# Second mixture of experts: router worked by chunks inside the last block, first expert's row by TensorE, accumulators opened early, chunks turned back through four banks

## Chip, cores and metric

One core of one Trainium2 chip runs the whole program as one launch. The metric is the device time of that launch in microseconds, before and after the change, as the median of several runs.

## The reference, cut to what matters

Two layers, each an attention part and an expert part, on 2048 tokens of width 128. The change is in the second layer, from the last block to the end, and in two places of the first layer's experts.

```python
# L1_attn: 8 blocks, scanned: linear attention, then feed forward, each with residual and layernorm
x = _layernorm(attn + residual, ln1_s, ln1_b)
h = gelu(x @ Wf1 + bf1); ff = gelu(h @ Wf2 + bf2)
x = _layernorm(ff + residual, ln2_s, ln2_b)
# L1_ffn: 8 experts, top 2 of a softmax router, no capacity
scores = softmax(x2d @ gate_w.T)
h = silu(xe @ w1[e]) * (xe @ w3[e]);  out = out + h @ w2[e]        # hidden width 352
# around them
x = x + ga * _L1_attn_ref(h, ...)
h = _layernorm(x, axis=-1) * (1 + cb) + sb
x = x + gb * _L1_ffn_ref(h, ...)
```

## The kernel before

The tokens are 16 tiles of 128, in four chunks (NC = 4) of four tiles. X and XN hold tokens on the partitions, HT holds features on the partitions. PS is the accumulator memory of TensorE, eight banks of 512 columns. Every engine has its own instruction stream, written out by hand in the order in which it runs; semaphores join them. Names: PE is TensorE, v is VectorE (DVE), a is ScalarE (ACT), g is GpSimd (POOL), sp is SyncE, which issues the loads and stores in its queue's order.

The last block (`pe_body`, `act_body`, `v_body`) goes through the chunks m = 0 to 3. A chunk has a first product with gelu (HF, `pe_f1`), a second (`pe_f2`), G2B from ScalarE, the sum Y2 on VectorE (L1927), four transposes to tokens (`pe_t2`), statistics (`v_stats`), the power -1/2 on GpSimd, the normalisation (`v_apply`), four transposes back (`pe_u2`) and scale and bias into HT (`act_x2`). The steps of one chunk's end lie between those of the next.

When all four chunks are in HT, the second expert part begins, with each step for all chunks before the next:

1. sixteen transposes of HT back to tokens (L1717) and the additions to X on VectorE (L2260);
2. the norm: statistics on VectorE (`norm_stats`), `norm_rstd` on GpSimd, `norm_apply` on ScalarE, four transposes into bank 7 (`norm_turn`), scale and bias into HT (`norm_feat`); bank 7 is one, so the chunks follow each other;
3. router products of all 16 tiles into bank 4 (`pe_router`), copied by VectorE (`v_logits`), then the choice of two experts on VectorE (`v_route1`), giving wt;
4. wt turned by TensorE, copied to wtT and stored to device memory (scr_w). Each expert's row of weights, 16 x 128 numbers, is then loaded from there to all partitions, into SB1 (`sp_row1`, 1 MB);
5. meanwhile TensorE opens the four accumulators with a product by zero (`pe_moe1`).

The loop over experts follows: GpSimd multiplies HT by the row into XS (L2046), TensorE makes the two products (L2074, L2075), ScalarE silu, VectorE the product HG, TensorE the third product into the accumulator of the chunk. 8 experts, 4 chunks and 3 pieces of hidden width make 96 tiles. At the end `act_back` copies the accumulators to OT, `pe_back` turns a chunk into bank 7 when VectorE has taken the one before, `v_last` adds it to X, and SP stores it.

The first layer's experts end in the same `pe_back`, and begin with `pe_route0` (one small product that counts tokens per expert) and `pe_row0`, by which the row of the first expert is spread by TensorE and copied by ScalarE and VectorE.

## Time and profile before

| | us |
|---|---|
| median of 3 runs | 2030.13 (2030.09 to 2036.85) |
| profiled execution, its own time | 2029.81 |
| its span | 2028.1 |
| TensorE busy | 1723.4 (85%) |
| VectorE busy | 1358.1 (67%) |
| ScalarE busy | 1159.0 (57%) |
| GpSimd busy | 290.5 (14%) |

The shares are means over stages that have different limits. The chain that ended last lies for 55% of the span on TensorE, 30% on VectorE, 7% on ScalarE and 3% in loads. Blocks run from about 1202 to 1715 us, the second expert loop from 1769 to 2018. Times below are from the start of the span, in us. A TensorE product in f32 with 512 columns appears as two instructions (two passes), a transpose as one.

### The profile page before, as it was taken

How to read it: one execution, taken by the hardware profiler on the slowest of the kernel's cores; microseconds unless marked ns; L12 is line 12 of the kernel's file. 1: busy time of each engine (PE TensorE's matmuls, PEld its weight loads, DVE VectorE, ACT ScalarE, POOL GpSimd, SP SyncE). 2: the span in 40 equal slices, each digit the busy share in tenths (PEclk: the TensorE clock that was granted, in tenths of full speed). 3: DMA queues.
4: the chain of work that ended last, by engine and by line, in shares of the span. 5: the costliest groups of instructions: out<-in, count | busy, mean ns of one | idle time of the engine just before them, and what ended most of it. 6: DMA issues, size and time to landing. Idle time of an engine off the chain costs nothing.

```text
span 2028.1 us, 28151 instructions
## 1 busy us (share of the span) xinstructions
PE 1723.4 (85%) x10382; PEld 768.5 (38%) x10382; DVE 1358.1 (67%) x2666; ACT 1159.0 (57%) x2106; POOL 290.5 (14%) x384
## 2 busy tenths in 40 slices
PE   5798058799999999999969948888988887499998
PEld 3798055122222222222344424444444443244443
DVE  6998876999999999999343355656656565122222
ACT  5565003298999999999823355666656664222222
POOL 4465002300000000000000021111111112011110
PEclk8999578599999999999979969999999999599999
DMA  1000000112000000000114200000000000211340
GB/s 50 1 2 1 0 0 9 48 31 38 2 2 2 2 2 1 2 2 2 33 33 88 68 0 1 16 16 16 16 1 16 16 0 1 59 36 46 49 58 25
DMA packets 74590, 40.15 MB, mean 20 GB/s; under 512 B 22128, under 2 KB 70768, under 8 KB 74464
## 3 DMA queue, kind: packets, MB, share of 16 engines
q1 hardware_dynamic: 73888, 37.70, 9.2%
q8 instruction: 77, 1.26, 0.3%
q10 hardware_dynamic: 576, 0.79, 0.1%
q14 instruction: 49, 0.40, 0.1%
HBM read 35.13 MB, written 3.15 MB: 19 GB/s over the span
## 4 chain that ended last, share of the span: by engine, by line
PE 55%; DVE 30%; ACT 7%; issue 4%; DMA 3%; SPq 1%; POOL 1%; DVEq 0%; ACTq 0%; POOLq 0%
DVE MX L1130 17%; PE PS L1642 6%; PE PS L1648 5%; PE PS L1212 5%; PE PS L2074 4%; PE PS L2075 4%; PE PS L2084 4%; PE PS L1238 3%; PE PS L1593 3%; DMA SB<-scr_w 3%; PE PS L525 2%; PE PS L1612 2%; PE PS L1089 2%; DVE MS L629 2%; PE PS L1484 2%
## 5 line engine op out<-in xcount | busy, mean ns | idle before, releaser
L1271 ACT ACTIVATE tmpb<-PS 128x512 f32<-128x512 f32 x1024 | 554.2, 595 | 75.6 <-PE PS L1238 56.5
L1130 DVE TENSOR_REDUCE MX<-PS 128x2 f32<-128x1024 f32 x512 | 584.4, 1215 | 17.6 <-PE PS L1089 15.5
L1212 PE MATMUL PS<-tmpb,VS 128*32 128x256 f32 x4096 | 327.7, 392 | 1.5 <-ACT tmpb L1271 0.6
L1089 PE MATMUL PS<-KST,QST 56*128 56x512 bf16 x1024 | 205.6, 400 | 18.5 <-DVE MX L1130 16.7
L1238 PE MATMUL PS<-QST,KST 59*128 59x512 bf16 x1024 | 200.5, 388 | 3.6 <-DMA QST<-NMP 0.6
L2109 DVE TENSOR_TENSOR HG<-HG,PS 128x512 f32<-128x512 f32 (+1 forms) x96 | 65.9, 686 | 199.5 <-PE PS L2075 199.5
L2099 ACT ACTIVATE HG<-PS 128x512 f32<-128x512 f32 (+1 forms) x96 | 57.2, 596 | 208.0 <-PE PS L2074 208.0
L1212 PEld LDWEIGHTS PS<-tmpb,VS 128*32 128x32 f32 x4096 | 80.8, 108 | 196.0 <-issue 108.0
L1238 PEld LDWEIGHTS PS<-QST,KST 59*128 59x128 bf16 x1024 | 49.4, 92 | 222.2 <-ACT tmpb L1271 208.8
L1642 PE MATMUL PS<-X,WF 128*128 128x512 f32 x256 | 128.3, 636 | 4.2 <-ACT X L1787 4.2
L1803 ACT ACTIVATE HF<-PS,CL 128x512 f32<-128x512 f32 x128 | 88.0, 687 | 68.5 <-PE PS L1642 68.5
L1648 PE MATMUL PS<-HF,WF 128*128 128x512 f32 x256 | 116.4, 592 | 0.0
L2074 PE MATMUL PS<-XS,G 128*128 128x512 f32 (+1 forms) x192 | 99.1, 597 | 12.2 <-POOLq L2048 12.2
L1900 DVE TENSOR_SCALAR N<-PS,BA,RR 128x128 f32<-128x128 f32 x256 | 85.9, 403 | 25.7 <-POOL RR L1946 14.4
L1927 DVE TENSOR_TENSOR Y<-G2B,X 128x512 f32<-128x512 f32 x32 | 22.1, 692 | 119.1 <-ACT G2B L1811 119.1
L2075 PE MATMUL PS<-XS,G 128*128 128x512 f32 (+1 forms) x192 | 98.6, 595 | 0.0
L2084 PE MATMUL PS<-HG,G 128*128 128x512 f32 (+1 forms) x192 | 96.8, 592 | 0.0
L525 PE MATMUL PS<-BIG,ident 128*128 128x128 f32 x512 | 66.5, 285 | 29.4 <-DVE BIG L460 29.4
L1593 PE MATMUL PS<-HT,WA 128*128 128x512 f32 x192 | 90.6, 605 | 0.1
L1507 DVE TENSOR_TENSOR HID<-HID,SB 128x512 f32<-128x512 f32 x64 | 42.6, 689 | 70.1 <-ACT HID L1496 38.4
L1184 POOL TENSOR_SCALAR NG<-MM 128x16 f32<-128x16 f32 x16 | 4.1, 254 | 550.0 <-DVE MM L1136 550.0
L1946 POOL TENSOR_TENSOR RR<-VE,mhalf 128x4 f32<-128x4 f32 x32 | 38.4, 1198 | 307.9 <-DVE VE L1893 307.9
(326 smaller groups left out, 2549.1 us busy)
## 6 DMA issues: line engine op xcount, KB each, us to landing
SB<-scr_w SPq DMA_DIRECT2D x15, 1024.0 KB, 14.9
WF<-in_L_attn_Wf SPq DMA_DIRECT2D x16, 256.0 KB, 3.0
QST<-NMP SPq DMA_DIRECT2D x192, 1.0 KB
G<-in_L_ffn_w SPq DMA_DIRECT2D x16, 176.0 KB, 2.4
W<-in_L_ffn_w SPq DMA_DIRECT2D x16, 128.0 KB, 2.1
QST<-scr_q SPq DMA_DIRECT2D x14, 128.0 KB
scr_q<-tmpb SPq DMA_DIRECT2D x3, 512.0 KB, 3.6
KST<-scr_k SPq DMA_DIRECT2D x14, 96.0 KB
```

The lines of the kernel that those rows point to most:

```text
L525: pe.matmul(PS[:, x, 0:HH * SCOL], ident[:, :], PR[:, i, heads(x), :].rearrange("p h c -> p (h c)"), start=i == 0, stop=False, skip_group_ ...
L1089: pe.matmul(PS[:, b + x, :], QST[r, 2 * g + jj, CH * qc + P * t:CH * qc + P * t + P], KST[r, g, cs(kc)], start=True, stop=True).then_inc(s ...
L1130: r = v.tensor_reduce(MX[:, :, m // (TPC * NC), m // NC % TPC, m % NC], PS[:, b:b + 2, :], AX.X, ALU.max)
L1212: last = pe.matmul(PS[32 * j:32 * j + 32, 3, h], VS[:, kt, u // NC, :], PB[:, kt % 2, j, h], start=(kt == 0 and half == 0), stop=(kt == NT ...
L1238: pe.matmul(PS[:, (at + x) % 3, :], KST[r, g, P * kt:P * kt + P], QST[r, 2 * g + jj, cs(qc)], start=True, stop=True).then_inc(s_qk, 1)
L1271: a.activation(PB[:, kt % 2, j, :], PS[:, at % 3, :], ACT.Exp, scale=HD ** -0.5).then_inc(s_exp, 1)
L1593: pe.matmul(PS[:, bank, :], WA[:, b % 2, j, :], HT[:, cs(c)], start=True, stop=True).then_inc(done, 1)
L1642: pe.matmul(PS[:, 3 + j % 2, :], WF1[:, b % 2, P * j:P * j + P], X1[:, n % 2, :], start=True, stop=True).then_inc(s_f1, 1)
L1648: f = pe.matmul(PS[:, 5, :], WF2[:, b % 2, j, :], HF[:, j, :], start=(j == 0), stop=(j == KF - 1))
L2074: pe.matmul(PS[0:w, b, :], G1[:, k, f:f + w], XS[:, c % 2, :], start=True, stop=True).then_inc(s_h, 1)
L2075: last = pe.matmul(PS[0:w, b + 1, :], G3[:, k, f:f + w], XS[:, c % 2, :], start=True, stop=True)
L2084: pe.matmul(PS[:, c, :], G2[0:w, k, m, :], HG[0:w, o % 4, :], start=False, stop=False, skip_group_check=True).then_inc(s_hfree, 1)
```

## The change

The chunks of the second expert part are worked inside the last block: transposes back (`pe_out1`), addition (`v_out1`), statistics (`v_stat1`), the power alone on GpSimd (`norm_pow`), the normalisation on VectorE (`v_norm_apply`), turning (`pe_turn1`), scale and bias (`act_feat1`) and router products (`pe_logits1`). The accumulators are opened right behind the router's last product (`pe_sums1`). The first expert's row is spread by TensorE (`pe_row`, now for both expert parts), so one row load falls away. `pe_back` uses the banks 4 to 7 for the chunks, in both expert parts. `pe_route0` gets three products whose result nobody reads. The gate's eight small loads stand earlier in SP's queue.

```diff
+        def norm_pow(g, S_, k, c):
+            g.wait_ge(S_["stat"], upto(k, c))
+            g.tensor_tensor(rs[:, ts_(c)], vh[:, ts_(c)], mhalf[:, ts_(c)], ALU.pow).then_inc(S_["rstd"], 1)
+
+        def v_norm_apply(v, S_, src, k, c):
+            v.wait_ge(S_["rstd"], upto(k, c))
+            for t in tiles(c):
+                last = v.tensor_scalar(XN[:, t, :], src[:, t, :], ag[:, t, 0:1], rs[:, t:t + 1], ALU.subtract, ALU.mult)
+            last.then_inc(S_["normed"], 1)
...
@@ def pe_route0
             pe.matmul(PS[:, 6, 0:8], below[:, :], r["two"][:, 0, :], start=True, stop=True).then_inc(r["s_cntd"], 1)
+            for _ in range(3):
+                pe.matmul(PS[:, 7, :], ident[:, :], HT[:, cs(0)], start=True, stop=True)
             pe_weights(pe, r)
...
@@ def pe_back
                 pe.wait_ge(s_oc, NC * n + c + 1)
-                if n or c:
-                    pe.wait_ge(s_y, NC * n + c)
                 for j, t in enumerate(tiles(c)):
-                    last = pe.transpose(PS[:, 7, P * j:P * j + P], OT[:, P * t:P * t + P], ident[:, :])
+                    last = pe.transpose(PS[:, 4 + c, P * j:P * j + P], OT[:, P * t:P * t + P], ident[:, :])
...
@@ def sp_blocks
+            for e in range(E1):
+                sp.dma_start(gate1[:, e:e + 1], A["L1_ffn_gate_w"][e].rearrange("(p a) -> p a", a=1)).then_inc(R1["s_in"], 16)
...
@@ def pe_body
                 else:
+                    if b == NB - 1:
+                        pe_out1(pe, 0)
                     pe_f2(pe, b, m, range(KF // 2))
                     pe_u2(pe, n + m - 1)
                     pe_f2(pe, b, m, range(KF // 2, KF))
                     if b < NB - 1:
                         pe_k(pe, b + 1, 0)
+                    else:
+                        pe_out1(pe, 1)
                 pe_t2(pe, n + m)
...
             else:
+                pe_turn1(pe, 0)
+                pe_out1(pe, 2)
+                pe_logits1(pe, 0)
+                pe_turn1(pe, 1)
                 pe_u2(pe, n + NC - 1)
+                pe_logits1(pe, 1)
+                pe_out1(pe, 3)
+                pe_turn1(pe, 2)
+                pe_logits1(pe, 2)
+                pe_turn1(pe, 3)
+                pe_logits1(pe, 3)
+
+        def pe_out1(pe, c):
+            pe.wait_ge(s_bx2, NC * (NB - 1) + c + 1)
+            if c == 3:
+                pe.wait_ge(s_x3, 1)
+            for j in range(TPC):
+                x = pe.transpose(PS[:, c % 3, P * j:P * j + P], HT[:, CH * c + P * j:CH * c + P * j + P], ident[:, :])
+            x.then_inc(s_bxt, 1)
...
@@ def v_body
+                if b == NB - 1 and m == NC - 1:
+                    v_out1(v, chain, 0)
+                    v_stat1(v, chain, 0)
+                    v_out1(v, chain, 1)
+                    v_norm_apply(v, SM, X, 5, 0)
                 v.wait_ge(s_g2, n + m + 1)
...
@@ def v_blocks
                 else:
+                    v_stat1(v, chain, 1)
                     v_stats(v, chain, 1, 6, s_t2, s_ep2, NC * NB - 1)
+                    v_norm_apply(v, SM, X, 5, 1)
                     v_apply(v, 1, 6, N2, s_r2, s_u2, s_n2, NC * NB - 1)
+                    v_out1(v, chain, 2)
+                    v_stat1(v, chain, 2)
+                    v_out1(v, chain, 3)
+                    v_stat1(v, chain, 3)
+                    v_norm_apply(v, SM, X, 5, 2)
+                    v_norm_apply(v, SM, X, 5, 3)
...
@@ sp_moe1
             sp_weights(sp, R1)
-            for k in range(2):
-                sp_row1(sp, k, k)
+            sp_row1(sp, 1, 1)
...
@@ tensor's program
             pe_blocks(pe)
-            for c in range(NC):
-                norm_turn(pe, SM, 5, c, (SM["feat"], 5 * NC + c) if c else (s_bx2, NC * NB))
-            pe_router(pe, R1, 6 * NC, 16 + 16 * E1)
+            pe_sums1(pe)
             pe_weights(pe, R1)
+            pe_row(pe, R1)
             pe_moe1(pe)
             pe_back(pe, 1, OT1)
```

The order of instructions shows it at three places. First TensorE in the last chunk of the last block, before the change. L1642 is the first product, L1648 the second, L1612 a turn of N (to features) or of Y (to tokens), L1717 the transposes back:

```order
L1642 MATMUL PS<-X,WF 128x512 [waits s_hf] x2
L1648 MATMUL PS<-HF,WF 128x512 [waits s_hf] x2
L1612 MATMUL PS<-ident,N 128x128 [waits s_bx2,s_n2]
L1612 MATMUL PS<-ident,N 128x128 x3
L1648 MATMUL PS<-HF,WF 128x512 [waits s_hf] x2
L1612 MATMUL PS<-ident,Y 128x128 [waits s_y2]
L1612 MATMUL PS<-ident,Y 128x128 x3
L1612 MATMUL PS<-ident,N 128x128 [waits s_bx2,s_n2]
L1612 MATMUL PS<-ident,N 128x128 x3
L1717 MATMUL PS<-ident,HT 128x128 [waits s_bx2]
L1717 MATMUL PS<-ident,HT 128x128 x3
```

And with the change, where L1716 is `pe_out1` and L1724 is `pe_turn1`:

```order
L1649 MATMUL PS<-X,WF 128x512 [waits s_hf] x2
L1716 MATMUL PS<-ident,HT 128x128 [waits s_bx2]
L1716 MATMUL PS<-ident,HT 128x128 x3
L1655 MATMUL PS<-HF,WF 128x512 [waits s_hf] x2
L1619 MATMUL PS<-ident,N 128x128 [waits s_bx2,s_n2]
L1619 MATMUL PS<-ident,N 128x128 x3
L1655 MATMUL PS<-HF,WF 128x512 [waits s_hf] x2
L1716 MATMUL PS<-ident,HT 128x128 [waits s_bx2]
L1716 MATMUL PS<-ident,HT 128x128 x3
L1619 MATMUL PS<-ident,Y 128x128 [waits s_y2]
L1619 MATMUL PS<-ident,Y 128x128 x3
L1724 MATMUL PS<-ident,XN 128x128 [waits s_normedM]
```

The transposes of chunks 0 and 1 now stand ahead of and behind the second product, and the first turn of the norm ahead of the last turn of N.

Second VectorE around the last Y2 sum, before:

```order
L1900 TENSOR_SCALAR N<-PS,BA,RR 128x128 x3
L1927 TENSOR_TENSOR Y<-G2B,X 128x512 [waits s_t2,s_g2]
L1888 BN_STATS BS<-PS 128x6 [waits s_t2]
L1888 BN_STATS BS<-PS 128x6 x3
L1891 BN_AGGR BA<-BS 128x2 [waits ch_v]
```

With the change, L2006 being `v_out1`, L130 to L140 the statistics and L160 the normalisation:

```order
L2006 TENSOR_TENSOR X<-X,PS 128x512 [waits s_bxt]
L130 BN_STATS st<-X 128x6 [waits ch_v]
L130 BN_STATS st<-X 128x6 x3
L133 BN_AGGR ag<-st 128x2 [waits ch_v]
L133 BN_AGGR ag<-st 128x2 x3
L140 TENSOR_SCALAR vh<-ag 128x4 [waits ch_v]
L2006 TENSOR_TENSOR X<-X,PS 128x512 [waits s_bxt]
L160 TENSOR_SCALAR XN<-X,ag,rs 128x128 [waits ch_v,s_rstdM]
L160 TENSOR_SCALAR XN<-X,ag,rs 128x128 x3
L1981 TENSOR_TENSOR Y<-G2B,X 128x512 [waits s_t2,s_g2]
```

Four steps (the addition of chunk 0, its statistics, the addition of chunk 1, the normalisation of chunk 0) stand ahead of the sum that the block waits for.

Third TensorE between router and expert loop, before (L1308 router, L1336 turn of wt, L2061 accumulators):

```order
L1308 MATMUL PS<-gate,HT 128x8 [waits s_featM,s_rin]
L1308 MATMUL PS<-gate,HT 128x8 x15
L1336 MATMUL PS<-ident,wt 128x128 [waits s_rw]
L2061 MATMUL PS<-zero,ident 128x512 [waits s_zero,s_rpd]
L2061 MATMUL PS<-zero,ident 128x512 x3
```

With the change (L1731 router, L2131 accumulators, L1337 turn of wt, L1456 the row):

```order
L1731 MATMUL PS<-gate,HT 128x8 x3
L2131 MATMUL PS<-zero,ident 128x512 [waits s_zero]
L2131 MATMUL PS<-zero,ident 128x512 x3
L1337 MATMUL PS<-ident,wt 128x128 [waits s_rw]
L1456 MATMUL PS<-wtT,ident 128x128 [waits s_rpd]
L1456 MATMUL PS<-wtT,ident 128x128 x15
L2138 UNCONDITIONAL_BRANCH [waits s_sb0]
```

The accumulators moved ahead of the routing's result, and sixteen products of the row came behind it.

## Rows read from the trace of the kernel before

**Rows 1.** The chain of waits, 1714 to 1771 us: start, length, engine, line.

```profile
1714.95 2.58 PE PS L1717 x12
...
1736.57 6.98 PE PS L1308 x32
...
1752.57 14.91 DMA SB<-scr_w
1767.55 1.27 POOL XS L2046
1769.01 2.04 PE PS L2074 x2
```

**Rows 2.** Busy time by stretch: PE, PEld, DVE, ACT, POOL, granted clock, DMA, GB/s.

```profile
1700.00:1760.00 60.00, 29.84 (x102) 19.52 (x101) 20.33 (x88) 17.22 (x30) 8.14 (x15) 0.66 0.12 28
```

**Rows 3.** TensorE in order of time, last chunk: start, length, line, operation, idle before.

```profile
1699.93 3.79 PE L1642 MATMUL PS<-X,WF 128*128 128x512 f32 x8
...
1705.71 1.88 PE L1648 MATMUL PS<-HF,WF 128*128 128x512 f32 x4
```

**Rows 4.** VectorE in order of time, last chunk and routing.

```profile
1708.35 0.69 DVE L1927 TENSOR_TENSOR Y<-G2B,X 128x512 f32<-128x512 f32 x1 [4.22 <-ACT G2B L1811]
1709.79 0.89 DVE L1888 BATCH_NORM_STATS2 BS<-PS 128x6 f32<-128x128 f32 x4 [0.75 <-PE PS L1612]
...
1712.42 1.37 DVE L1900 TENSOR_SCALAR N<-PS,BA,RR 128x128 f32<-128x128 f32 x4 [1.12 <-POOL RR L1950]
...
1743.57 0.29 DVE L1316 COPY L<-PS 128x128 f32<-128x128 f32 x1 [19.05 <-PE PS L1308]
...
1749.75 0.29 DVE L1997 TENSOR_TENSOR wt<-one,m 128x128 f32<-128x128 f32 x1
```

**Rows 5.** ScalarE and GpSimd in order of time, two steps of the passage.

```profile
1735.65 0.78 ACT L172 ACTIVATE HT<-PS,modc 128x512 f32<-128x512 f32 x1 [1.27 <-PE PS L166]
...
1711.37 1.01 POOL L1950 TENSOR_TENSOR RR<-VE,mhalf 128x4 f32<-128x4 f32 x1 [8.64 <-DVE VE L1893]
```

**Rows 6.** TensorE and VectorE in order of time, first experts' routing.

```profile
1038.64 0.39 PE L1413 MATMUL PS<-two,below 128*128 128x8 f32 x2 [1.51 <-DVEq L1396]
1041.54 0.40 PE L1336 MATMUL PS<-ident,wt 128*128 128x128 f32 x1 [2.51 <-DVE wt L1407]
1042.50 6.68 PE L1453 MATMUL PS<-wtT,ident 128*128 128x128 f32 x32 [0.55 <-DVEq L1342]
1050.11 3.67 PE L1477 MATMUL PS<-HT,W 128*128 128x512 f32 x8 [0.93 <-DVE SB L1463]
...
1041.19 0.29 DVE L1407 TENSOR_TENSOR wt<-t,m 128x128 f32<-128x128 f32 x1
```

**Rows 7.** VectorE and ScalarE in order of time, ends of both expert parts.

```profile
1166.21 0.69 DVE L2246 COPY Y<-PS 128x512 f32<-128x512 f32 x1 [3.25 <-PE PS L1520]
...
1171.81 0.69 DVE L2246 COPY Y<-PS 128x512 f32<-128x512 f32 x1 [1.33 <-PE PS L1520]
...
2018.13 2.42 ACT L1527 ACTIVATE OT<-PS,modc 128x512 f32<-128x512 f32 x4 [2.84 <-PE PS L2084]
...
2019.57 0.69 DVE L2116 TENSOR_TENSOR X<-X,PS 128x512 f32<-128x512 f32 x1 [3.26 <-PE PS L1520]
...
2024.98 0.69 DVE L2116 TENSOR_TENSOR X<-X,PS 128x512 f32<-128x512 f32 x1 [1.27 <-PE PS L1520]
```

**Rows 8.** GpSimd in order of time, first multiplication of the seventh expert.

```profile
1950.83 1.27 POOL L2046 TENSOR_TENSOR XS<-HT,SB 128x512 f32<-128x512 f32 x1 [10.36 <-DMA SB<-scr_w]
```

**Rows 9.** Busy time by stretch of 2 us, columns as in group 2.

```profile
1040.00:1042.00 2.00, 0.40 (x1) 0.14 (x1) 1.33 (x7) 0.00 (x0) 0.00 (x0) 0.92 0.00 0
1042.00:1044.00 2.00, 1.50 (x7) 1.51 (x8) 0.27 (x1) 0.00 (x0) 0.00 (x0) 0.50 0.11 33
...
1716.00:1718.00 2.00, 2.00 (x12) 1.77 (x10) 1.67 (x3) 0.00 (x0) 0.00 (x0) 0.62 0.00 0
1738.00:1740.00 2.00, 2.00 (x11) 2.00 (x11) 0.00 (x0) 0.00 (x0) 0.00 (x0) 0.50 0.00 0
```

More of the change, by code:

```diff
@@ L1292, in router @@
             r.update({n: sb(f"{n}{tag}", [P, NT], F32, stack) for n in ("m", "k")})
-            if nth == 1:
-                r["gate"], r["L"] = gate0, logit0
-            else:
-                r["gate"] = sb(f"gate{tag}", [P, E], F32, stack)
-                r["L"] = sb(f"L{tag}", [P, NT, E], F32, stack)
+            r["L"] = logit0 if nth == 1 else sb(f"L{tag}", [P, NT, E], F32, stack)
             r["wtT"] = sb(f"wtT{tag}", [P, P], F32, stack)
@@ L1301, in router @@
             return r
-        def pe_router(pe, r, feat, arrived):
-            pe.wait_ge(r["s_in"], arrived)
-            pe.wait_ge(SM["feat"], feat)
-            for t in range(NT):
-                last = pe.matmul(PS[:, 4, 8 * t:8 * t + 8], HT[:, P * t:P * t + P], r["gate"][:, :], start=True, stop=True)
-            last.then_inc(r["s_mm"], 1)
         def bc(ap):
@@ L1686, in pe_body, with pe_turn1, pe_logits1 @@
             else:
+                pe_turn1(pe, 0)
+                pe_out1(pe, 2)
+                pe_logits1(pe, 0)
+                pe_turn1(pe, 1)
                 pe_u2(pe, n + NC - 1)
+                pe_logits1(pe, 1)
[11 more added lines that the diff above has]
+            x.then_inc(s_bxt, 1)
+        def pe_turn1(pe, c):
+            pe.wait_ge(SM["normed"], upto(5, c))
+            if c >= 2:
+                pe.wait_ge(SM["feat"], upto(5, c - 2))
+            for j, t in enumerate(tiles(c)):
+                x = pe.transpose(PS[:, 3 + c % 2, P * j:P * j + P], XN[:, t, :], ident[:, :])
+            x.then_inc(SM["turned"], 1)
+        def pe_logits1(pe, c):
+            pe.wait_ge(R1["s_in"], 16 + 16 * E1)
+            pe.wait_ge(SM["feat"], upto(5, c))
+            for t in tiles(c):
+                x = pe.matmul(PS[:, 5, E1 * t:E1 * t + E1], HT[:, P * t:P * t + P], gate1[:, :], start=True, stop=True)
+            if c == NC - 1:
+                x.then_inc(R1["s_mm"], 1)
         def pe_inputs(pe, b):
@@ L1713, in pe_blocks @@
                 pe_body(pe, b)
-            for c in range(NC):
-                pe.wait_ge(s_bx2, NC * (NB - 1) + c + 1)
-                for j in range(TPC):
-                    x = pe.transpose(PS[:, c, P * j:P * j + P], HT[:, CH * c + P * j:CH * c + P * j + P], ident[:, :])
-                x.then_inc(s_bxt, 1)
         KGROUPS = (slice(0, 1), slice(1, 3), slice(3, 4))
@@ L1823, in act_blocks, with act_feat1 @@
                 else:
+                    act_feat1(a, 0)
+                    act_feat1(a, 1)
                     act_x2(a, b, NC - 1)
+                    act_feat1(a, 2)
+                    act_feat1(a, 3)
+        def act_feat1(a, c):
+            a.wait_ge(SM["turned"], upto(5, c))
+            a.activation(HT[:, cs(c)], PS[:, 3 + c % 2, :], ACT.Identity, scale=modc[:, 1, 4:5], bias=modc[:, 1, 3:4]).then_inc(SM["feat"], 1)
         def v_k(v, chain, b, g):
@@ L2020, in sp_moe1 @@
         def sp_moe1(sp):
-            for e in range(E1):
-                sp.dma_start(R1["gate"][:, e:e + 1], A["L1_ffn_gate_w"][e].rearrange("(p a) -> p a", a=1)).then_inc(R1["s_in"], 16)
             for k in range(2):
@@ L2169, in _ @@
             g.memset(zero[:, :], 0.0).then_inc(s_zero, 1)
-            for c in range(NC):
-                norm_rstd(g, chain, SM, 5, c, False)
             g.wait_ge(SM["feat"], 6 * NC)
@@ L2193, in _ @@
             act_blocks(a, Chain(a, ch_a))
-            for c in range(NC):
-                norm_apply(a, SM, X, 5, c)
-                norm_feat(a, SM, 5, c, modc[:, 1, 4:5], modc[:, 1, 3:4])
             act_route1(a, R1)
+            for c in (0, 2):
+                act_row(a, R1, SB1, c)
             act_moe1(a)
@@ L2210, in _ @@
             pe_route0(pe, R0)
-            pe_row0(pe, R0)
+            pe_row(pe, R0)
             pe_moe0(pe)
@@ L2257, in _ @@
             v_blocks(v, chain)
-            for c in range(NC):
-                v.wait_ge(s_bxt, c + 1)
-                v.tensor_tensor(X[:, ts_(c), :], X[:, ts_(c), :], PS[:, c, :].rearrange("p (t d) -> p t d", t=TPC),
-                                ALU.add).then_inc(s_x3, 1)
-            v.wait_ge(s_x3, NC)
-            for c in range(NC):
-                norm_stats(v, chain, SM, X, c, 1e-5, False)
             v_route1(v, chain, R1)
+            for c in (1, 3):
+                v_row(v, R1, SB1, c)
             v_moe1(v)
```

48 lines of the change are left out of this document (31 added, 17 removed).

## Prediction

> **What bounds the kernel now.** I read the chain of waits first, then each engine in order of time between 1698 and 1772 us, then the granted clock of that stretch. The span is 2028.1 us, the profiled execution's own time 2029.81, so 1.7 us lie around the span; the median of the runs shown is 2030.13, 0.3 above it. Inside the blocks and inside the expert loops the change moves nothing, so only four seams count: the start and the end of the first experts' loop, the passage from the last block to the second experts' loop, and the end of the kernel.
>
> The passage is the large one. The last feed-forward product of the blocks ends near 1707.6 [rows 3], and the second experts' first product starts at 1769.01 [rows 1]. In between TensorE is busy half of the time at a mean clock of 0.66 [rows 2]. The chain runs through sixteen transposes, norm statistics, four rounds of "normalise, turn, scale" one after another, 6.98 us of router products, 6.5 us of routing on VectorE (copy at 1743.57, weights ready at 1749.75 + 0.29 = 1750.04) [rows 1, 4], a write to device memory, and then 14.91 us in which everything waits for the first expert's row of weights [rows 1]. No other wait of the passage is so long.
>
> **Part by part. First the passage as far as the router's result.** Before, VectorE stands idle for 4.22 us ahead of the last Y2 sum at 1708.35 [rows 4]. The change puts chunks 0 and 1 there. TensorE turns chunk 0 back behind the first product of chunk 3, four transposes: 0.86 us at half clock (2.58 for twelve [rows 1]), 0.44 at full, so the second product ends 0.44 later. VectorE adds chunk 0 from about 1704.4 (0.69, the same form as the adds of [rows 7]) and takes its statistics (1.5 us, from 1709.79 until GpSimd starts at 1711.37 [rows 4, 5]), to 1706.6. The addition of chunk 1 waits for its transposes, which stand behind the second product: about 1708.6 to 1709.3. Then chunk 0 is normalised on VectorE. Four tensor_scalar of 128x128 take 1.37 us from PSUM [rows 4]; this form, with SBUF as source, isn't in the trace, so I bound it by that row above and, below, by the 0.69 that one instruction over the same 512 elements takes [rows 7], and take 1.1, nearer to the four short ones. Y2 therefore starts near 1710.4: 2.05 us late, and who waits for it is the last chunk of the block. Its statistics stand behind those of chunk 1 too (1.5 us) and start near 1712.6 against 1709.79; after GpSimd (1.0 [rows 5]) and the normalisation of chunk 1, its own follows at 1715.15 against 1712.42 [rows 4]: the block's last chunk is 2.7 us late.
>
> From there two things run beside each other. TensorE has by then had little to do and I expect the half clock: four transposes 0.86 us, router products of a chunk 1.75 (6.98 / 4). TensorE: turn of chunk 1 to 1716.2, the last chunk's turn to 1717.6, router products of chunk 1 to 1719.4, and only then the transposes of chunk 3, to 1720.4. VectorE: add to 1721.3, statistics to 1722.8, normalise chunk 2 to 1723.9 and chunk 3 to 1724.9. Last come turn (0.9 and 0.2 of latency), scaling on ScalarE (0.78 [rows 5]) and router products (1.75) of chunk 2, then the same of chunk 3: the scaling of chunk 3 waits for a turn that stands behind chunk 2's router products. 1723.9 + 1.1 + 0.8 + 1.8 + 1.1 + 0.8 + 1.8 is 1731.3. VectorE copies the logits at 1731.4 instead of 1743.57: **12.2 us**. At full clock all of this tail would end near 1727.2, for 16.3.
>
> **The accumulators.** Four zero products (eight passes, 3.8 us at full clock by the row at 1699.93 [rows 3], twice that at half) now lie beside the 6.5 us of routing. If the clock rises in the middle they are done before the weights, else up to 0.7 us late. I take 0.1.
>
> **The first row by TensorE.** Before, from weights ready to first product: 1769.01 - 1750.04 = 18.97 us [rows 1, 4]. The first experts' loop already does what is now planned: weights ready 1041.48, first product 1050.11, so 8.63 us [rows 6]; here GpSimd's multiplication is added (1767.55 to 1769.01: 1.46 [rows 1]), 10.1 together. That is with 32 row passes in 6.68 us at half clock (granted clock 0.50 from 1042 [rows 6, 9]). At full clock they take half, and the whole 6.8. The zero products keep TensorE busy until 1 or 2 us before the weights are ready, so I take the full clock: 18.97 - 6.8, **12.1 us**; at half 8.9.
>
> **Start of the loop.** It opens at half clock: the first pair of passes takes 2.04 us [rows 1], where a quarter of [rows 3]'s eight is 0.95. About 1.8 us are lost before the clock rises. Now row passes run until 2.4 us ahead of it. I take half, **0.9**, bounds 0 and 1.8.
>
> **Three warming products in the first routing.** TensorE has only 0.39 us of work at 1038.64 between two idle times of 1.5 and 2.5 us, and the clock falls just before the row passes (0.92 on average in 1040 to 1042, 0.50 after) [rows 6, 9]. Three products are six passes, 2.6 us at full clock: they begin at about 1038.9 and end at 1041.5, when the weights are ready (1041.48). The passes then take 3.4 instead of 6.68: **3.2 us**. If the clock fell all the same the gain is 0; if the warming products ran at half clock they would end at 1044.0 and cost 2.5. The loop behind depends on row loads that its own progress issues, so it moves as a whole.
>
> **Four banks instead of one.** After the first experts VectorE copies the four chunks from 1166.21 on, the last at 1171.81 [rows 7], so 1.9 us apart on average, since TensorE waits for each copy. With four banks they follow each other at 0.7, so the last starts at 1168.3: **3.5 us**, all on the path to the norm. At the end of the kernel likewise: ScalarE's four copies end at 2020.55, VectorE's sums start at 2019.57 and 0.65 apart, the last at 2021.5 instead of 2024.98 [rows 7]: 3.5. The four stores of the output get closer together; what stands between the last sum and the end (2028.1 - 2025.67 = 2.4) may grow a little: **3.4**.
>
> **Costs of nothing.** The gate's eight loads leave the queue of SP between chunk and expert loads and go ahead of block 2, where SP waits for the blocks anyway. GpSimd loses the negated means; its zero fill stays hidden under the norms. The copies to SBUF of the row are in the 8.63.
>
> Sum: 12.2 - 0.1 + 12.1 + 0.9 + 3.2 + 3.5 + 3.4 = 35.2; 2029.8 - 35.2 = 1994.6, plus 0.3 for the median: **1995**.
>
> **Rivals.** (a) *The clock lets a row down.* Idle times of 1 to 2.4 us stand ahead of each row and of the loop; an idle of 2.5 next to a short product was enough for the fall at 1041 [rows 6, 9]. If the second row and the loop's start stay at half: 3.2 + 0.9 less, 1999; the first row too: 2002. (b) *The tail runs at full clock*, 4.1 more: 1991. For it: in 1716 to 1718 TensorE ran only transposes and the granted clock went from its lower to its upper level (mean 0.62) [rows 9]. Against it: in 1738 to 1740 it was busy all the time with router products and stayed at 0.50 [rows 9], and these now stand between the transposes. The Trainium skill, "TensorE: Matmul & The Clock Gate", Part 4 (PE-mode transpose), says that transposes don't count as work for the clock; by that rule (b) could not be at all and the sum would be as above. The trace disagrees, by the rise at 1716 to 1718. (c) *Filling VectorE's gap delays the block more than I reckon*: if the additions wait for one another so that chunk 3's transposes come 6 us later than I have them, the passage gives 6 and the time is 2001. (d) *Slower: the second loop waits for its rows.* The row of a later expert is ready for use at 1950.83 + 1.27 = 1952.1 [rows 8], its products start 72 tiles behind 1769.01, a tile being (2018.13 - 1769.01) / 96 = 2.59 [rows 1, 7], so near 1956: 4 us to spare. The loads must each take 4 + 35/6 us longer than now, about 10 on top of 15, to use up the gain over six loads, and 12 to make it 0.5% slower. Two rows issued together had the first at 14.91 [rows 1]; now that pair is gone, so contention falls. (e) *Nothing gained*: another load takes the place of the row's 14.91 us. The weights of the first two experts are asked for when chunk 3 is added (1721) and needed at 1744.7. For no change they would have to land 30 us after that, over 50 us after their issue, three times what the row's load takes.
>
> **Chances.** Forecast 0.55; (a) 0.24; (b) 0.09; (c) 0.07; (d) 0.02; (e) 0.03. The forecast's own bounds: 0.9 up and down at the loop's start, 1 on the normalisation, 1 for where a clock change falls: 1991 to 1998. To leave out no more than 2 in 10 the range takes (a) and most of (b) and (c): 1989 to 2003. Some 0.5% (10 us) is what a measurement of this kernel can tell from no change; faster by more than that are the forecast and (a) to (c), 0.95; within it 0.03; slower 0.02.
>
> **What would show it.** Right: row passes behind both routings at 0.11 us each; no DMA wait on GpSimd ahead of the second loop's first XS; logits copied some 24 us after the last block's second product and not 36; VectorE's four sums at either end 0.7 apart. Wrong: passes of 0.21 at either row (a); TensorE at 1.00 through the tail (b); the last Y2 over 3 us late or a long wait of the sum of chunk 3 (c); TensorE idle inside the second loop, behind GpSimd (d); a wait for G ahead of it (e). The forecast fails most easily at the tail, which I laid out instruction by instruction, and at the clock, which no row shows for these mixtures of work.

## Result and the profile after

The changed kernel took 2000.24 us (median of 4 runs, 1998.69 to 2001.04) where the kernel before took 2030.89 on the same chip (4 runs, 2030.09 to 2036.85): the ratio is 0.9842, 95% interval 0.9822 to 0.9862. That is 30.7 us less; the forecast was 35, with 1995 as the time and 1989 to 2003 as its range. The profiled execution took 1998.69, its span is 1997.0, 31.1 below that of before.

The page of the changed kernel, busy time by engine:

```profile
PE 1726.2 (86%) x10420; PEld 769.0 (39%) x10420; DVE 1363.9 (68%) x2684; ACT 1154.2 (58%) x2092; POOL 288.9 (14%) x376
```

TensorE and VectorE, on which most of the chain lies, have a little more to do than before (2.8 and 5.8 us); ScalarE has 4.8 us less, since the second norm is now applied on VectorE. The gain is idle time. I divided both spans into the same eleven stretches (at the start times of named instructions in the timelines of the engines; the weights and the Y copies at their end) and subtracted. "Logits copied" is the start of the copy. Each column is one execution. All in us:

```
stretch                                            before   after   change  forecast
start -> first routing's weights ready            1041.48 1041.75   +0.27     0
 -> first product of the first experts' loop         8.63    5.71   -2.92    -3.2
 -> OT copies (the loop)                           114.76  115.49   +0.73     0
 -> last of VectorE's four Y copies has ended        7.63    4.56   -3.07    -3.5
 -> first product of the blocks (the norm)          29.85   29.84   -0.01     0
 -> first product (f1) of the last chunk           497.58  498.53   +0.95     0
 -> logits copied (the passage)                     43.64   31.47  -12.17   -12.2
 -> second routing's weights ready                   6.47    6.47    0        0
 -> first product of the second experts' loop       18.97    7.10  -11.87   -12.0
 -> OT copies (the loop)                           249.12  249.28   +0.16    -0.9
 -> end                                              9.97    6.80   -3.17    -3.4
```

The chain of waits of the changed kernel through the second routing's end:

```profile
1725.47 1.86 PE PS L1731 x8
1727.35 0.30 DVE L L1317
...
1733.53 0.30 DVE wt L2072
...
1734.75 3.85 PE PS L1456 x32
1738.69 0.70 DVE SB L1470
1739.46 1.27 POOL XS L2118
1740.92 1.38 PE PS L2149 x2
1742.30 1.71 PE PS L2150 x2
```

Where [rows 1] had 14.91 us of DMA there are 3.85 us of TensorE and a copy. The router products of a chunk are a piece of their own now, 1.86 us for eight, and only the last chunk's stand in the chain behind the last turn.

VectorE in order of time around the last Y2 sum:

```profile
1704.45 0.69 DVE L2006 TENSOR_TENSOR X<-X,PS 128x512 f32<-128x512 f32 x1 [1.98 <-PE PS L1716]
1705.29 1.11 DVE L160 TENSOR_SCALAR XN<-X,ag,rs 128x128 f32<-128x128 f32 x4 [0.16 <-DVE X L2006]
1706.32 0.69 DVE L1981 TENSOR_TENSOR Y<-G2B,X 128x512 f32<-128x512 f32 x1
...
1710.97 1.37 DVE L1949 TENSOR_SCALAR N<-PS,BA,RR 128x128 f32<-128x128 f32 x4
...
1716.24 0.69 DVE L2006 TENSOR_TENSOR X<-X,PS 128x512 f32<-128x512 f32 x1 [1.66 <-PE PS L1716]
```

The last chunk's f1 starts at 1699.93 before [rows 3] and at 1695.88 now. From it the Y2 sum starts 10.44 us later and not 8.42: 2.02 late, forecast 2.05. The last apply of N starts 15.09 later against 12.49 [rows 4]: 2.6, forecast 2.7. Normalising with SBUF as source takes 1.11 for four, as taken. The gap of 4.22 of [rows 4] is filled but for 1.98 ahead of chunk 1's addition, which waits for its transposes.

VectorE in order of time, after the first experts and at the end of the kernel:

```profile
1164.30 3.21 DVE L2317 COPY Y<-PS 128x512 f32<-128x512 f32 x4 [3.25 <-PE PS L1525]
...
1991.63 2.48 DVE L2191 TENSOR_TENSOR X<-X,PS 128x512 f32<-128x512 f32 x4 [3.26 <-PE PS L1525]
```

Four copies are one group without idle time between them, where [rows 7] has them 1.87 us apart.

### The profile page after: what moved, and what is told of

Its sections match the earlier page's. It is cut to its first block, busy times and chain, and to the rows that moved or that the text cites. A ratio compares the mean times of both kernels' runs of the same rounds, so it can differ in the third digit from the quotient of the medians.

```text
span 1997.0 us, 28224 instructions
## 1 busy us (share of the span) xinstructions
PE 1726.2 (86%) x10420; PEld 769.0 (39%) x10420; DVE 1363.9 (68%) x2684; ACT 1154.2 (58%) x2092; POOL 288.9 (14%) x376
## 4 chain that ended last, share of the span: by engine, by line
PE 56%; DVE 30%; ACT 6%; issue 4%; DMA 2%; SPq 1%; POOL 1%; DVEq 0%; ACTq 0%; POOLq 0%
DVE MX L1143 17%; PE PS L1649 6%; PE PS L1655 6%; PE PS L1225 5%; PE PS L2149 4%; PE PS L2150 4%; PE PS L2159 4%; PE PS L1251 4%; PE PS L1600 3%; PE PS L538 2%; PE PS L1619 2%; PE PS L1491 2%; PE PS L1484 2%; PE PS L1102 2%; DVE MS L642 2%
## 5 line engine op out<-in xcount | busy, mean ns | idle before, releaser
L1649 PE MATMUL PS<-X,WF 128*128 128x512 f32 x256 | 128.4, 636 | 4.2 <-ACT X L1828 4.2
```

The source lines that it names most:

```text
L1649: pe.matmul(PS[:, 3 + j % 2, :], WF1[:, b % 2, P * j:P * j + P], X1[:, n % 2, :], start=True, stop=True).then_inc(s_f1, 1)
```

## Experiments

Each edit is made to the changed kernel, unless it says otherwise. Times are medians; the kernel before ran beside each. The changed kernel itself was timed twice: 2000.24 above and 2001.33 below, 0.9842 and 0.9841 of the kernel before. The first four runs share a chip, and so do the next four and the last three; the kernel before had medians of 2034.2, 2030.47 and 2031.13 there, so ratios compare across the groups and times do not. In brackets behind a ratio is its 95% interval. Only three of the ratios lie clear of the changed kernel's: the row by load again (slower) and the two kernels with products in every block (faster). The other runs are read by their stretches, each from one profile. "Stretch" means a row of the table above.

**Row by TensorE without the warming products.**

```diff
-            for _ in range(3):
-                pe.matmul(PS[:, 7, :], ident[:, :], HT[:, cs(0)], start=True, stop=True)
```

> The changed kernel without the three warming products in the first routing. Theory (they hold TensorE's clock up for the row passes): the 32 row passes of the first experts take about 6.7 us instead of 3.84 and the first product comes 2.5 to 3 us later; time about 2.5 us above the changed kernel, near 2003. Rival (the clock would have been up anyway, so they do nothing): row passes stay at 3.8 and the time at 2000.

Measured: 2003.6 (2003.2 to 2003.66, 4 runs), 0.9849 [0.9832, 0.9865]. TensorE in order of time, in the first routing:

```profile
1040.81 0.39 PE L1414 MATMUL PS<-two,below 128*128 128x8 f32 x2 [0.23 <-DVEq L1397]
1043.72 0.47 PE L1337 MATMUL PS<-ident,wt 128*128 128x128 f32 x1 [2.52 <-DVE wt L1408]
1044.74 6.26 PE L1454 MATMUL PS<-wtT,ident 128*128 128x128 f32 x32 [0.55 <-DVEq L1343]
```

The changed kernel, same place:

```profile
1042.69 3.84 PE L1456 MATMUL PS<-wtT,ident 128*128 128x128 f32 x32 [0.55 <-DVEq L1343]
```

The idle 2.52 us is back and 32 passes take 6.26 for 3.84; from weights to first product it is 8.26 for 5.71. So the products without use are worth 2.55 us in this run, through the clock: the granted clock of 1040 to 1046 is 1.00 in the changed kernel, and here 0.50 from 1044 to 1048. All stretches behind differ by under 0.1 us each. The time alone (0.9849 for 0.9842) would not show this gain.

**The first row of the second experts by load again.**

```diff
-            sp_row1(sp, 1, 1)
+            for k in range(2):
+                sp_row1(sp, k, k)
...
-            pe.wait_ge(s_sb0[0], 4 * NC)
...
-            pe_row(pe, R1)
+            pe.wait_ge(R1["s_pd"], 2)
...
-            for c in (0, 2):
-                act_row(a, R1, SB1, c)
...
-            for c in (1, 3):
-                v_row(v, R1, SB1, c)
```

> The changed kernel with the first expert's row of the second experts loaded from device memory again, two row loads issued together. Theory (the load's 15 us were all on the path): from weights ready to first product about 19 us against 7.1, time 12 us above the changed kernel, near 2012. Rival (part of the load would lie under the earlier weights and accumulators): less than 8 us above.

Measured: 2011.96 (2009.91 to 2017.05, 4 runs), 0.9896 [0.9876, 0.9916]. The stretch from weights to first product is 19.21, 12.1 more than in the changed kernel. Its chain of waits:

```profile
1735.70 15.29 DMA SB<-scr_w
...
1751.06 1.27 POOL XS L2119
...
1752.52 2.05 PE PS L2149 x2
```

The load is on the path with its full length, and no other load takes its place when it goes.

**One bank in place of four**, at the end of both expert parts.

```diff
-                    last = pe.transpose(PS[:, 4 + c, P * j:P * j + P], OT[:, P * t:P * t + P], ident[:, :])
+                    last = pe.transpose(PS[:, 7, P * j:P * j + P], OT[:, P * t:P * t + P], ident[:, :])
```

and a wait ahead of it for VectorE to have taken the chunk before, as the kernel before has.

> The changed kernel with the turn back through bank 7 alone at both places. Theory (each turn waits for VectorE's read of the one before): 3.1 us more behind the first experts and 3.2 us more at the end, 6.2 in all, near 2006.5. Rival (VectorE and the stores would pace the ends anyway): under 3 us more.

Measured: 2007.3 (2005.83 to 2008.37, 4 runs), 0.9865 [0.9849, 0.9882]. The two stretches take 2.97 and 3.67 us more (7.53 and 10.47), 6.6 together, and each sum waits for its own transposes. TensorE and VectorE in order of time at the end:

```profile
1998.10 0.63 PE L1527 MATMUL PS<-ident,OT 128*128 128x128 f32 x4 [0.87 <-DVE X L2193]
1998.77 0.69 DVE L2193 TENSOR_TENSOR X<-X,PS 128x512 f32<-128x512 f32 x1 [0.81 <-PE PS L1527]
1999.60 0.69 PE L1527 MATMUL PS<-ident,OT 128*128 128x128 f32 x4 [0.87 <-DVE X L2193]
2000.33 0.69 DVE L2193 TENSOR_TENSOR X<-X,PS 128x512 f32<-128x512 f32 x1 [0.87 <-PE PS L1527]
```

**The chunks after the block, not inside it.** All of the norm, turns and router products still go by chunks, but behind the last apply of the block.

```diff
@@ pe_body
-                    if b == NB - 1:
-                        pe_out1(pe, 0)
...
-                    else:
-                        pe_out1(pe, 1)
...
+                pe_u2(pe, n + NC - 1)
+                pe_out1(pe, 0)
+                pe_out1(pe, 1)
+                pe_out1(pe, 2)
                 pe_turn1(pe, 0)
-                pe_out1(pe, 2)
@@ v_body
-                if b == NB - 1 and m == NC - 1:
-                    v_out1(v, chain, 0)
-                    v_stat1(v, chain, 0)
-                    v_out1(v, chain, 1)
-                    v_norm_apply(v, SM, X, 5, 0)
```

The same steps stand behind `v_apply` and `act_x2` of the last chunk on the other engines.

> The changed kernel with the norm and router still worked chunk by chunk and normalised on VectorE, but all of it behind the block's last chunk; nothing stands ahead of the last Y2 sum. Theory (most of the 12.2 us of the passage comes from the shorter pipeline of chunks, the rest from VectorE's idle time inside the block): the last Y2 sum comes 1.6 us earlier, the logits are copied 2 to 4 us later than in the changed kernel; time 2002 to 2004. Rival (the gain is the work hidden inside the block): 8 us or more later, 2008 and above. Third possibility (the delay of Y2 costs more than the filling gives): same time or lower.

Measured: 2006.61 (2006.11 to 2009.43, 4 runs), 0.9868 [0.9852, 0.9884]. VectorE in order of time:

```profile
1704.85 0.69 DVE L1974 TENSOR_TENSOR Y<-G2B,X 128x512 f32<-128x512 f32 x1 [4.22 <-ACT G2B L1850]
...
1708.92 1.37 DVE L1947 TENSOR_SCALAR N<-PS,BA,RR 128x128 f32<-128x128 f32 x4 [1.12 <-POOL RR L2017]
```

The gap and the early Y2 sum (8.42) are back as before, and yet the passage is 38.43, 6.96 longer than in the changed kernel and 5.21 shorter than before. So of the 12.17 us of the passage 7.0 come from work put inside the block, the delay of the block already paid, and 5.2 from taking the chunks one behind the other instead of step by step. The run takes all of that work out of the block: what fills VectorE's gap ahead of the Y2 sum, and also what stands behind the sum, among the last chunk's steps. How much the gap alone gives it doesn't show. Both theories missed (2 to 4 us later, or 8 and more). TensorE's clock falls 11.7 us behind f1 here and 11.6 in the changed kernel, so the two passages are compared at the same clock.

**Three seams: products without use and an earlier row load.**

```diff
                 for k in range(2):
-                    sp.wait_ge(s_ewfree, k + 2)
-                    sp_expert0(sp, i * 2 + (k + 2), k)
                     sp.wait_ge(s_sbfree, k + 1)
                     sp_row(sp, r, i * 2 + (k + 2), k)
+                    sp.wait_ge(s_ewfree, k + 2)
+                    sp_expert0(sp, i * 2 + (k + 2), k)
...
+            for _ in range(2):
+                pe.matmul(PS[:, 0, :], ident[:, :], zero[:, :], start=False, stop=False, skip_group_check=True)
             pe.wait_ge(s_sb0[0], 4 * NC)
...
                 norm_turn(pe, S4, 4, c, (S4["feat"], c) if c else (s_y, NC))
+                if c < NC - 1:
+                    pe.matmul(PS[:, 6, :], ident[:, :], Y[:, 0:TPC, :].rearrange("p t d -> p (t d)"), start=True, stop=True)
```

> The changed kernel with three edits in three places far apart, each read in its own stretch. (1) Two products by zero between the second row's passes and the second experts' loop. Theory (the 2.3 us idle there let the clock fall at 1741.6, and the loop opens at half clock): the loop from first product to the copies of the accumulators takes 247.5 to 248 us instead of 249.28. Rival (the fall comes from what happened earlier): 249.3. (2) One product between the turns ahead of the blocks, in place of idle time. Theory: the first block's first products run at full clock, blocks 1 to 3 us shorter than 498.5. Rival: two more short products don't lift it, 498.5. (3) In the first experts' loop the row's load is issued ahead of the weights' loads. Theory (the loop loses 4 to 5 us to rows that land late, and the 0.7 us by which the loop grew in the changed kernel is such a wait): 110.5 to 112 us instead of 115.5. Rival: 115.5. Together 1990 to 1995 by the theories, 2000 by the rivals.

Measured: 1995.59 (1993.49 to 1997.58, 4 runs), 0.9836 [0.982, 0.9853]. The second loop takes 247.58 for 249.28. TensorE in order of time at the loop's start, this kernel:

```profile
1737.59 1.10 PE L2151 MATMUL PS<-XS,G 128*128 128x512 f32 x2 [0.61 <-POOLq L2120]
```

and the changed one:

```profile
1740.92 1.38 PE L2149 MATMUL PS<-XS,G 128*128 128x512 f32 x2 [2.33 <-POOLq L2120]
1742.09 1.92 PE L2150 MATMUL PS<-XS,G 128*128 128x512 f32 x2
```

With the idle time down to 0.61 the loop runs at full clock; two of eight profiles without these products did so too (below). The products between the norm's turns ahead of the blocks show no effect: the blocks' first 24 passes take 12.12 us, and 11.74 to 13.03 in the profiles without them; the 1 to 3 us hoped for in the blocks did not come (497.7 for 498.53). With the row load ahead of the weights the first loop takes 113.93, 1.6 less than in the changed kernel but only 0.5 below the shortest of the profiles with the old order (114.40 to 116.26), and not the 110.5 to 112 that I had expected. VectorE's waits for rows (26.0 us in five in the changed kernel) are gone, and waits for weights have come in their place:

```profile
1087.72 1.12 PE L1484 MATMUL PS<-HT,W 128*128 128x512 f32 x2 [1.12 <-DMA W<-in_L_ffn_w]
```

**Products without use in the tail.** `pe_fill` is a product of the identity with HT into a free bank, without a reader.

```diff
                         pe_out1(pe, 1)
+                        pe_fill(pe, 3)
...
                 pe_out1(pe, 3)
+                pe_fill(pe, 2)
                 pe_turn1(pe, 2)
```

> The changed kernel with three idle products ahead of the turn of the last Y2 and two ahead of the turn of chunk 2. Theory (the tail from the last chunk to the logits runs at half clock because TensorE waits twice for some 3 us, and full clock is worth up to 4 us): tail 28 to 29.5 us instead of 31.47, time 1997 to 1998. Rival (the short products of router and turns keep the clock down whatever is put between, or the idle products delay more than they give): tail 31 to 32.5, time 2000 to 2001.

Measured: 1996.41 (1994.39 to 1996.5, 4 runs), 0.9834 [0.9818, 0.985]. Busy time by stretch (PE, PEld, DVE, ACT, POOL, granted clock, DMA, GB/s):

```profile
1704.00:1711.00 7.00, 5.88 (x31) 3.65 (x29) 5.92 (x28) 1.46 (x2) 1.78 (x2) 1.00 0.00 0
1711.00:1714.00 3.00, 2.40 (x11) 2.00 (x11) 2.71 (x9) 0.91 (x2) 0.26 (x1) 0.53 0.02 5
1714.00:1718.00 4.00, 4.00 (x14) 2.97 (x14) 2.36 (x12) 0.65 (x1) 1.01 (x1) 0.50 0.00 0
1718.00:1721.00 3.00, 1.58 (x6) 0.51 (x5) 2.71 (x14) 0.58 (x1) 1.51 (x2) 1.00 0.85 239
1721.00:1724.00 3.00, 2.66 (x12) 2.35 (x12) 0.00 (x0) 0.19 (x1) 0.00 (x0) 0.57 0.37 121
```

The clock rises where the last two products stand, and falls again as chunk 2's router products begin. Chunk 0's eight router passes took 1.03 us at full clock, the others 1.72 to 1.85; but they took 1.03 in the changed kernel's repetition too, which has no such products. The passage is 30.69, above the 28 to 29.5 of the theory. With the same tail code and no products in it, it was 31.47 in the changed kernel's profile, 31.46 without the warming products, 30.39 with the row by load, 30.34 with one bank and 30.62 in the repetition. So this run doesn't show a gain in the passage. The products did not carry the full clock through the router products of chunks 2 and 3.

**The last Y2 sum ahead of chunk 1's addition**, so that the block's last chunk is less late. With it, and not shown below, TensorE takes the last chunk's turn ahead of chunk 1's and chunk 3's transposes ahead of chunk 1's router products, and ScalarE and GpSimd follow that order.

```diff
                     v_stat1(v, chain, 0)
-                    v_out1(v, chain, 1)
-                    v_norm_apply(v, SM, X, 5, 0)
                 v.wait_ge(s_g2, n + m + 1)
...
                 else:
-                    v_stat1(v, chain, 1)
+                    v_out1(v, chain, 1)
+                    v_norm_apply(v, SM, X, 5, 0)
                     v_stats(v, chain, 1, 6, s_t2, s_ep2, NC * NB - 1)
-                    v_norm_apply(v, SM, X, 5, 1)
+                    v_stat1(v, chain, 1)
                     v_apply(v, 1, 6, N2, s_r2, s_u2, s_n2, NC * NB - 1)
+                    v_norm_apply(v, SM, X, 5, 1)
```

> The changed kernel with the addition and normalisation of chunk 1 and 0 behind the last Y2 sum instead of ahead, the last chunk's statistics ahead of chunk 1's, and chunk 3's transposes ahead of chunk 1's router products. Theory (Y2 comes 2.0 us late, and the last chunk's path to its addition sets the end): Y2 8.8 us behind the chunk's first product instead of 10.44, tail 1.5 to 2.5 us shorter, 29 to 30. Rival (VectorE is the bound of the tail, so the order moves nothing): tail 31 to 32.

Measured in one run: 2000.53. The Y2 sum starts 8.85 us after f1 and not 10.44; the passage is 29.82, 0.5 to 1.6 below the others with the old order, by all these moves together. That the time doesn't show it fits the blocks, 502.0 in this run, of which below.

**Accumulators behind the row.**

```diff
-            pe_sums1(pe)
             pe_weights(pe, R1)
             pe_row(pe, R1)
+            pe_sums1(pe)
```

> The changed kernel with the accumulators opened behind the row passes. Theory (beside the routing they cost nothing and they keep the clock up for the row): the row passes take about 6.3 instead of 3.84, and from weights ready to first product 11 to 14 us instead of 7.10, since four products of zero now stand between. Rival (the clock is up anyway by then): row passes 3.84 and 8.6 to 9 us.

Measured in one run: 1997.16. TensorE in order of time:

```profile
1732.26 5.56 PE L1456 MATMUL PS<-wtT,ident 128*128 128x128 f32 x32 [0.55 <-DVEq L1343]
1737.65 3.60 PE L2131 MATMUL PS<-zero,ident 128*128 128x512 f32 x8
```

The row passes open at half clock, behind 6.55 us of idle time with one short turn after it; the first product comes 9.91 us after the weights and not 7.10 (11 to 14 was expected). Of these 2.8 us 1.7 are the row's passes and 1.1 the zero products' place on the path. But the zero products now keep TensorE busy up to the loop, which takes 247.51 for 249.28. Beginning the accumulators early is worth 1.0 us net here, and 2.8 in an execution in which the loop would have stayed at full clock anyway.

**Products without use in every block.** In the traces above the first product of a chunk, eight passes at L1649, took 3.86 us in some blocks and over 5 in others. TensorE waits 2.75 us for the apply of N ahead of it.

```diff
             pe_wo(pe, b, 3)
+            for _ in range(2):
+                pe.matmul(PS[:, 0, :], ident[:, :], HT[:, cs(0)], start=True, stop=True)
             pe_u1(pe, n)
```

> The changed kernel with two idle products in each of the eight blocks, ahead of the first turn of N, where TensorE waits 2.7 us for VectorE. Theory (in some blocks the clock falls there and the first product of the block takes 5.6 to 5.8 us instead of 3.86, so that the eight blocks take 497.6 to 502 us by where the clock's changes fall; this is most of the 1 us that the blocks of the changed kernel lost against the kernel before, and of the spread of the runs): blocks 488 to 492 us against 498.5, time 1991 to 1994. Rival (the length of the blocks has another cause, or the idle products delay the chain): 498 or more, time 2000.

Measured: 1988.4 (1987.01 to 1990.75, 5 runs), 0.9786 [0.9771, 0.9802]. TensorE in order of time in the second block, first the changed kernel:

```profile
1286.25 0.66 PE L1619 MATMUL PS<-ident,N 128*128 128x128 f32 x4 [2.75 <-DVE N L1949]
...
1287.86 5.44 PE L1649 MATMUL PS<-X,WF 128*128 128x512 f32 x8 [0.52 <-ACT X L1828]
```

and with the two products:

```profile
1286.21 0.66 PE L1619 MATMUL PS<-ident,N 128*128 128x128 f32 x4 [1.04 <-DVE N L1951]
...
1287.83 3.86 PE L1649 MATMUL PS<-X,WF 128*128 128x512 f32 x8 [0.52 <-ACT X L1830]
```

All eight blocks show 3.86 now, the blocks take 490.76 us, as expected (488 to 492), and the time is below the 1991 to 1994 of the theory. In the changed kernel four of eight were 5.44 to 5.55, as in the kernel before (5.41 to 5.55), and in its repetition seven of eight 4.42 to 5.90. Of the 7.8 us by which the blocks are shorter than in the changed kernel these rows are 6.6; 1.2 lie in the blocks' first 24 passes (11.74 for 12.93), ahead of the products.

**The best of it together**: the block's products, those ahead of the second loop, the row load first, and the Y2 sum first.

> The changed kernel with what paid in the earlier runs: the idle products in the blocks, the two products by zero ahead of the second experts' loop (1.7 us), the row load ahead of the weights' loads in the first experts (1.6), and the last Y2 sum first (0.5 to 1.6). Theory (these lie in different stretches and add up): 6 to 10 us from the blocks and 4 from the rest, 1984 to 1989. Rival (only the last three count): 1995 to 1997.

Measured: 1987.33 (1985.85 to 1988.15, 5 runs), 0.9778 [0.9763, 0.9793]. Its shorter stretches (first loop 113.32, Y2 8.85, passage 29.82) stand against blocks of 492.04, and its interval overlaps the one above: the block's two products are all that is shown to matter.

**The changed kernel again**, on the same chip as the two above.

> The changed kernel itself, as the reference on this chip for the two others: 1999 to 2003.

Measured: 2001.33 (1994.79 to 2003.2, 5 runs), 0.9841 [0.9821, 0.986], blocks 503.46. The two filled kernels are 13 to 14 us faster than this, with intervals clear of its own.

## Why the prediction was right, and its sizes

**The passage (forecast 12.2, measured 12.17).** Right, step by step: Y2 2.02 late, last apply 2.6 late, chunk 3's sum 20.4 us behind f1 (forecast 20.7), logits 31.47 behind f1 (forecast 31.47). The run with the chunks behind the block shows that 7.0 of it are the work put inside the block. The half clock through the tail, on which the sum rested, held in this profile: 0.50 in each stretch of 2 us in which the router products ran.

That the sizes agree to 0.03 us is luck. Eight profiles have the same tail code (the changed kernel and its repetition, and the runs without warming products, with the row by load, with one bank, with three seams, with late accumulators and with the blocks filled). Their passages took 31.47, 30.62, 31.46, 30.39, 30.34, 30.30, 30.30 and 31.23 us. The shorter ones have a part of the tail at full clock. With the row by load TensorE ran nothing but twelve transposes from 1707.65 to 1710.5, and then chunk 0's router products at full clock:

```profile
1710.58 1.03 PE L1731 MATMUL PS<-gate,HT 128*128 128x8 f32 x8
```

```profile
1708.00:1710.00 2.00, 2.00 (x11) 2.00 (x10) 1.90 (x14) 0.35 (x1) 0.93 (x1) 0.50 0.00 0
1710.00:1712.00 2.00, 1.89 (x15) 1.42 (x13) 1.83 (x11) 0.43 (x1) 1.11 (x2) 0.87 0.04 8
```

So the passage gains 12.2 to 13.3 against the one profile of the kernel before, by where the clock changes.

**The first row by TensorE (forecast 12.1, less 0.1 for the accumulators; measured 11.87).** Right, and the clock held: 3.85 us for 32 passes. The run with the load back shows the same 12.1 from the other side. From weights to first product it is 7.10 where the forecast had 6.8: 32 passes at full clock take 3.84 and not the 3.4 of half of [rows 6].

**The first row's warming products (3.2, measured 2.92).** Right; off by the same 3.84. The six passes without use took 2.82 and not the 2.6 reckoned, and ended just behind the weights.

**Four banks (3.5 and 3.4, measured 3.07 and 3.17).** Right. The copies to Y follow each other at 0.84 us (four start to end in 3.21), not at 0.7. At the end of the kernel the sums are 0.60 apart, as fast as reckoned; there the 0.2 lie behind them, in the stores: from the last sum's end to the end of the span it is 2.9 us now and was 2.4, where the forecast had allowed 0.1. One bank again costs 2.97 and 3.67.

**Start of the second loop (0.9 gained, measured 0.16 lost).** This term failed. I took half of 1.8, on the ground that row passes now run until 2.4 us ahead of it. The granted clock of the changed kernel (columns as above):

```profile
1738.00:1740.00 2.00, 0.59 (x6) 0.39 (x4) 0.69 (x1) 1.67 (x2) 0.54 (x1) 1.00 0.32 82
1740.00:1742.00 2.00, 1.08 (x2) 0.49 (x3) 0.00 (x0) 0.00 (x0) 1.82 (x2) 0.90 0.21 66
1742.00:1744.00 2.00, 2.00 (x4) 0.88 (x3) 0.00 (x0) 0.60 (x1) 0.17 (x1) 0.50 0.25 74
```

TensorE stands idle for 2.33 us, opens the loop at full clock, and the clock falls after the first passes, with the loop already running. The loop then took 249.28 us, as in six of the eight profiles with this idle time and the accumulators ahead of it; in two (products without use in the tail, and in the blocks) it took 247.58, as in both with the products ahead of the loop. So the term is 1.7 or nothing from one execution to the next. With products ahead of the loop 1.7 came both times, which by two of eight could still be chance. Rival (a) named this fall, but together with the second row's, which did not come.

**The blocks and the first loop (0, measured +0.95 and +0.73).** "Inside the blocks and inside the expert loops the change moves nothing" is true of instructions and not of time. With the same instructions the blocks took 497.6 to 503.5 us in the profiles, and the first loop 114.4 to 116.3. The 0.95 of this pair of profiles lies where the blocks begin. TensorE in order of time, before and in the changed kernel:

```profile
1202.35 12.04 PE L1593 MATMUL PS<-HT,WA 128*128 128x512 f32 x24
```

```profile
1197.35 12.93 PE L1600 MATMUL PS<-HT,WA 128*128 128x512 f32 x24
```

The same passes take 0.89 more, since the granted clock is at half for the first 4.9 us of them and not for 3.1. The spread up to 503.5 has its larger part at another place, and there the runs show the cause: the clock falls about TensorE's idle 2.75 us ahead of the first product of some blocks (four of eight before and now, seven in the repetition), and two products without use in that gap take this loss away. For the first loop I have no run that shows it; what I have is that it waits for row or weight loads whichever of them goes first.

The terms that fell short sum to the difference: row 0 0.3, first routing and loop 1.0, banks 0.7, blocks 0.9, passage and row 1 0.2, loop start 1.1: 4.1 of 35.2, of which 2.0 (first routing, loop, blocks) lie within what unchanged code varies by, and the loop start's 1.1 too. Nine executions of the changed kernel took 1994.79 to 2003.2 us; the range of the forecast, 1989 to 2003, holds all but the longest, and a nearer hit than some 4 us is luck.

**The rivals.** (a) fell: both rows ran at full clock, at 0.12 us a pass. (b) fell in this profile, where the tail ran at half; five profiles of the same tail gained 0.9 to 1.2 of its 4.1 us. (c) fell: chunk 3's transposes came in time. (d) and (e) fell: behind the routing no load stands in the chain, and the second loop is as long as before but for the clock.

The rule that stood against (b) gave the right sum for this tail, but these runs don't bear it out. The Trainium skill, "TensorE: Matmul & The Clock Gate", Part 4 (PE-mode transpose), says that the full clock doesn't engage for transposes, which don't count as busy in the same way. The rise from half to full clock at 1716 to 1718, with nothing but transposes on TensorE (mean 0.62), speaks against it [rows 9], and so does the rise at 1710 to 1712 with the row by load, behind twelve transposes.

## What to carry to other kernels

Work that only the next stage needs can go inside a stage with idle gaps, even if it delays that stage a little: here 7.0 us were gained after 2.6 us of delay were paid. A row of 16 x 128 numbers that all partitions need is spread by sixteen products in 3.8 us at full clock (5.6 to 6.7 where they began at half), where its store and load took 1.57 and 15.29. And where TensorE waits ahead of dense products, compare the first of them in every repetition: if it takes over a third longer in some, two products without a reader in the gap may be worth more than a restructured stage (here 13 us in the medians).

## What the runs showed of the hardware

The clock's fall depends on the execution. Behind the same idle 2.75 us, the same eight passes took 3.86 in some blocks and up to 5.90 in others, and which blocks it was changed from one profile to the next with equal instructions there. The chain of waits of the changed kernel in two neighbouring blocks:

```profile
1287.86 5.44 PE PS L1649 x8
...
1351.72 3.86 PE PS L1649 x8
```

The Trainium skill, "TensorE: Matmul & The Clock Gate", Part 1 (The HAM clock gate), says that what a kernel loses to the half clock differs from run to run with equal code; the traces agree, by 497.6 to 503.5 us for the same eight blocks.

The fall can show only once the work has begun again. In the block of 5.44 us the granted clock is 1.00 from 1283 to 1287, through the idle time, and 0.66 on average from 1287 to 1292, with the dense products; at the second loop it is 0.90 in the 2 us in which the idle time ends and 0.50 after. It can also come inside the idle time. In the repetition, ahead of a block whose first product took 5.71, TensorE stands idle from 1473.6 to 1476.35:

```profile
1474.00:1475.50 1.50, 0.00 (x0) 0.00 (x0) 0.60 (x3) 0.31 (x1) 0.89 (x1) 1.00 0.01 5
1475.80:1476.30 0.50, 0.00 (x0) 0.00 (x0) 0.49 (x2) 0.00 (x0) 0.00 (x0) 0.50 0.00 0
```

So a full clock throughout the idle time doesn't show that the idle time is harmless: look at the rows behind it.

And router products stayed at half clock though TensorE had no break: 0.50 from 1738 to 1740 before [rows 9]. In the run with the filled tail the mean clock went from 1.00 to 0.57 with the stretch in which chunk 2's began, after 1 us of idle time. A chunk of them takes 1.85 us there and 1.03 at full clock. Two of the four chunks are on the path behind the last chunk's sum, and in all profiles of this tail these two ran at half.
